# A new order for the first stage of an attention and mixture-of-experts layer, with routing spread over the shared expert by a table

## The chip, the core and the metric

The kernel runs on one core of a Trainium2 chip. The metric is the time of one execution on the device, in microseconds (us), as the median of several runs. PE is TensorE, DVE is VectorE, ACT is ScalarE, POOL is GpSimd and SP is SyncE, which here only issues DMAs. Each engine executes its own queue in order, and waits in it on semaphores.

## The reference

```python
xn = layernorm(x)                       # x is 4 x 1024 tokens of 256
z = softmax((xn@Wq.T + bq) @ (xn@Wk.T + bk).T / 16) @ (xn@Wv.T + bv)      # per batch
gates = softmax(xn @ Wg.T)              # 16 experts, the best 2 chosen, their scores normalised
y = sum over the 2 of score * ((silu(xn@We_gate.T) * (xn@We_up.T)) @ We_down.T)   # hidden 128
shared = (silu(xn@Ws_gate.T) * (xn@Ws_up.T)) @ Ws_down.T                   # hidden 512
out = x + z + y + sigmoid(xn@Wsg.T) * shared
```

## The kernel before

The 4096 tokens are 32 tiles of 128 and 8 chunks of 512 tokens (4 tiles). All wide products are made in three passes: each operand is split in a rounded part (HI, a copy by ACT) and the remainder (LO, a subtraction, `remainder`, by DVE), and PE multiplies HI by HI, HI by LO and LO by HI.

There are three stages. **Stage one** is the shared expert of all 8 chunks, with the layer norm, the routing, and the splitting of all expert weights beside it. **Stage two** takes 40 pairs of blocks of 128 tokens, each block for one expert; it begins when PE starts line 847 (`blk_gate_up`, 0). **Stage three** is the attention, with the scattered results of the experts gathered and added. The change touches the first stage and small things that follow from it.

`plan()` writes out one list of steps, and each engine's program walks it and executes its own share of each step. So a step's place in the list is its place in all queues. The steps of stage one are:

- `stats c`: DVE's statistics of a chunk's 4 tiles; `root`, `invert`: DVE and ACT make the reciprocal deviation, for the groups of chunks in `ROOTS`; `norm c`: the normalised tiles, two by POOL and two by ACT (chunk 0: two by DVE), which SP also stores to the tensor `rows`.
- `tokens_in c`: PE transposes the chunk (8 transposes, banks 0 and 1), ACT and DVE split the result into `xT`; SP stores it as `keys` at the step `logits c`.
- `logits c`: PE's router product (4 matmuls of 512 columns), ACT copies it out; `logits_turn c`: PE transposes it back, all into bank 7; `best_experts q` (two chunks each): DVE copies and adds the two halves, then `max` and `max_index` of 8 tiles.
- `gate_up c,j` (j from 0 to 3): two products, 12 matmuls of 512 columns, into banks 2 and 3 or 4 and 5; ACT takes the silu of the one, DVE multiplies it by the other (line 1195); `hidden c,j`: ACT (HI) and DVE (LO, line 1123) split it into `hT`. `down c,m`: 24 matmuls of 256 columns, and DVE adds the result (line 1209). The loop over these is called the shared sequence here, 48 parts; (c,j) is one of them.
- `row_shift`: 12 matmuls of one column from Wq and the biases; `shared_weights n`: the split of 512 columns of the shared weights.
- `chosen`, `counts`, `ranks`, `slot_sums`, `slots`, `slot_parts`: from the chosen experts to each token's slot, a chain between DVE and PE. `slot_hots g`: for 4 tiles, DVE compares the slots' places and blocks with a range (`place_hot`, `block_hot`, lines 1301 and 1297), POOL multiplies `block_hot` by the token numbers (line 623), and `rows_map g` on PE multiplies the two; 8 groups. Then the block's rows are known, and POOL may gather them (`blk_load`).
- `expert_split n`: HI by ACT, LO by DVE; SP loads expert n+2 when the LO of n is done (two staging buffers).

In the version before the order follows from rules (`expert_next`, `map_next`, `shared_next`): the logits steps and best experts stand between two parts, the routing chain behind (3,1), and an expert split behind each `gate_up` from then on, all 16 LO parts on DVE. The first `gate_up` stands behind two chunks of `tokens_in` and four of the six weight splits.

Of the kernel before, what the change touches and what calls it, by code (L numbers as in the profile page):

```python
# [18 lines left out]
P = 128  # L19
# [26 lines left out]
def shape_constants():  # L46
# [17 lines left out]
        (P * np.arange(TILES)[None, :] + p[:, None] - MIDDLE).astype(np.float32),  # L64
# [5 lines left out]
ORDER = [*range(4), *range(12, NE), *range(4, 12)]  # L70

AWAY = range(2, 6)
QT = TILES // 4
PER = P // NE
ROOTS = ((0,), (1,), (2, 3), (4, 5, 6, 7))


def plan():


    steps, held, unsplit, unmapped = [], [], list(range(NE)), list(range(-1, MAPS + 1))
    known = {"slots": False, "blocks": False}
# [5 lines left out]
    def expert_next(c):  # L88
        if not unsplit or not known["slots"]:
            return  # L90
        expert = ORDER[unsplit[0]]
        if expert >= 12:
            now = known["blocks"]
        elif expert >= 10:
            now = not unmapped
        elif expert >= 8:
            now = c > 5
        elif expert >= 6:
            now = c > 4
        elif expert >= 4:  # L100
            now = c > 3
        else:
            now = True
        if now:
            steps.append(("expert_split", unsplit.pop(0)))
# [20 lines left out]
    def shared_next():  # L126
        part, c, n = shared.pop(0)
        part(c, n)

    def map_next():  # L130
        g = unmapped.pop(0)
        if 0 < g:
            steps.append(("rows_map", g - 1))
        if g + 1 < MAPS:
            steps.append(("slot_hots", g + 1))
        if not unmapped:
            steps.append(("rows_known",))

    def normed_root(*chunks):
        steps.append(("root", *chunks))  # L140
        steps.append(("invert", *chunks))

    steps.append(("stats", 0))
    normed_root(0)
    steps += [("norm", 0), ("stats", 1)]
    normed_root(1)
    steps += [("norm", 1), ("tokens_in", 0), ("row_shift",), ("shared_weights", 0), ("shared_weights", 1), ("stats", 2),
              ("shared_weights", 2), ("shared_weights", 3), ("stats", 3), ("tokens_in", 1)]
    normed_root(2, 3)
    steps += [("norm", 2), ("logits", 0), ("shared_weights", 4), ("shared_weights", 5)]  # L150
    shared_next()
    steps += [("logits_turn", 0), ("logits", 1)]
    for c in range(2, NCH + 1):
        if c < NCH:
            steps.append(("tokens_in", c))
        if c < 4:
            steps += [("stats", 2 * c), ("stats", 2 * c + 1)]
        if c == 3:
            normed_root(4, 5, 6, 7)
        if c + 1 < NCH:  # L160
            steps.append(("norm", c + 1))
        shared_next()
        if c > 2:
            steps.append(("logits", c - 1))
        shared_next()
        steps.append(("logits_turn", c - 1))
        if c % 2 == 0:
            steps.append(("best_experts", c // 2 - 1))
    steps.append(("chosen",))
    shared_next()  # L170
    shared_next()
    steps += [("counts",), ("expert_load", 0), ("expert_load", 1)]
    shared_next()
    steps += [("ranks",), ("slot_sums",)]
    shared_next()
    steps += [("slots",), ("slot_parts",)]
    known["slots"] = True
    for n in range(6):
        shared_next()
        if n % 2 == 0:  # L180
            map_next()
    steps += [("row_slots",), ("experts_of_blocks",), ("pair_scores",)]
    known["blocks"] = True
    while shared:
        shared_next()
        if unmapped:
            map_next()
        if shared:
            shared_next()
    while unsplit:  # L190
        expert_next(NCH)
    assert not unmapped

    steps += [("blk_load", b) for b in range(XR)]
    steps += [("blk_turn", 0), ("blk_turn", 1), ("down", NCH - 1, 0), ("down", NCH - 1, 1), ("qkv_load",)]
# [38 lines left out]
class Places:  # L234
# [3 lines left out]
    def __init__(self, steps):  # L238
# [4 lines left out]
        ring, turn, summed = 0, 0, False  # L243
        for step in steps:
            kind = step[0]
            banks = []
            if kind == "tokens_in":
                banks = [(("turn", (turn + k) % 2), (*step, k)) for k in range(KD)]
                turn += KD
            elif kind in ("logits", "rows_map"):  # L250
# [6 lines left out]
            elif kind == "down":  # L257
                banks = [(("down", step[2] if summed else 0), step)]
            elif kind == "slot_sums":
# [33 lines left out]
def build(nc, x, bv, Wqkv, bqk_in, Wr, We, Ws, const_f, const_b, out):  # L293
# [4 lines left out]
    with ctx:  # L298
# [206 lines left out]
        def inverse_of(c):  # L505

            return 5 * [c in group for group in ROOTS].index(True) + 4
# [17 lines left out]
        def sync_program(e):  # L525
# [10 lines left out]
            for c in range(3):  # L536
                load_x(c)
# [928 lines left out]
```

## Time and profile before

| | us |
|---|---|
| median of 3 runs (592.13 to 593.46) | 592.26 |
| the profiled execution's own time | 590.49 |
| its span, from the first to the last instruction | 588.7 |
| PE busy in the span | 542.5 |
| DVE busy in the span | 378.6 |
| start of stage two (PE line 847) | 209.04 |

The span leaves out what lies around the instructions (1.8 us here). Busy times are sums of an engine's instructions; PE's are modelled at their ends. Stages two and three are executed by the same code before and after the change.

### The profile page before, as it was taken

The numbers are of one execution on the slowest core, as the hardware profiler recorded it, in microseconds if no ns is written. First come the engines' busy times: TensorE is split into PE (matmuls) and PEld (weight loads), VectorE is DVE, ScalarE is ACT, GpSimd is POOL, SyncE is SP. The second block draws the span as 40 slices with busy tenths as digits, with TensorE's granted clock in tenths as the row PEclk, the third lists the DMA queues.
The fourth block names the chain that finished last, engine by engine and source line by source line (L and its number), as shares of the span: only waits on it lengthen the run. The fifth ranks groups of instructions, "written<-read, shape, count | busy, mean of one in ns | idle before, by whom it ended". The sixth has DMA issues, their size and how long they took to land.

```text
span 588.7 us, 10343 instructions
## 1 busy us (share of the span) xinstructions
PE 542.5 (92%) x3660; PEld 492.3 (84%) x3661; DVE 378.6 (64%) x798; ACT 233.3 (40%) x409; POOL 183.0 (31%) x174
## 2 busy tenths in 40 slices
PE   1595999797999999999999999999999999999997
PEld 1474878576888899999999889889888989889986
DVE  4576564689887557566665566665666656665665
ACT  3354442141454336555554533333333333333331
POOL 2123300012333467577760202222222222222222
PEclk9998999999899999999999999999999999999999
DMA  8752453012314156496676901115111111112112
GB/s 303 247 215 99 186 225 117 1 36 73 106 55 144 47 162 189 153 316 211 189 144 154 330 28 46 47 53 188 53 55 50 49 46 46 55 45 64 55 60 67
DMA packets 35600, 69.30 MB, mean 118 GB/s; under 512 B 4960, under 2 KB 17632, under 8 KB 34528
## 3 DMA queue, kind: packets, MB, share of 16 engines
q1 hardware_dynamic: 28064, 49.42, 23.8%
q0 software_dynamic: 6912, 18.88, 12.5%
q8 instruction: 31, 0.51, 0.4%
q10 hardware_dynamic: 576, 0.35, 0.2%
q14 instruction: 17, 0.14, 0.1%
HBM read 41.37 MB, written 27.26 MB: 117 GB/s over the span
## 4 chain that ended last, share of the span: by engine, by line
PE 80%; DVE 13%; ACT 3%; issue 2%; DMA 1%; POOL 0%; DVEq 0%; ACTq 0%
PE ps L669 46%; PE ps L847 10%; PE ps L791 7%; PE ps L868 5%; PE ps L675 5%; PE ps L923 5%; DVE bn_stats_out L1130 2%; PE ps L747 1%; DVE sil L1195 1%; DVE idx L1173 1%; DVE pT L1123 1%; DVE nmax L1403 1%; DMA acc<-in_x 1%; ACT vv L944 1%; DVE hT L1123 1%
## 5 line engine op out<-in xcount | busy, mean ns | idle before, releaser
L656 POOL DMA_INDIRECT rows_y<-ytab,slot x64 | 64.8, 1013 | 209.6 <-DVE acc L1432 179.5
L669 PE MATMUL ps<-xT,shared_w 128*128 128x512 f32 x384 | 96.2, 406 | 5.8 <-DVE sil L1195 5.8
L642 POOL DMA_INDIRECT blk_x<-rows,row x80 | 82.0, 1025 | 51.3 <-issue 26.4
L669 PEld LDWEIGHTS ps<-vv,pT 128*128 128x128 f32 x768 | 95.9, 192 | 1.9
L669 PE MATMUL ps<-vv,pT 128*128 128x256 f32 x768 | 97.0, 283 | 0.0
L669 PEld LDWEIGHTS ps<-xT,shared_w 128*128 128x128 f32 x384 | 74.2, 197 | 22.4 <-issue 6.0
L669 PE MATMUL ps<-xbT_hi,qT 128*128 128x512 f32 x256 | 87.5, 403 | 0.0
L1110 ACT ACTIVATE probs_f<-ps,less 128x1024 f32<-128x1024 f32 x32 | 35.7, 1115 | 103.8 <-DVE less L1406 103.8
L847 PE MATMUL ps<-expert_w,blk_xT 128*128 x480 | 66.6, 288 | 0.0
L847 PEld LDWEIGHTS ps<-expert_w,blk_xT 128*128 128x128 f32 x480 | 59.7, 190 | 0.1
L669 PEld LDWEIGHTS ps<-xbT_hi,qT 128*128 128x128 f32 x256 | 48.1, 188 | 9.4
L791 PE MATMUL ps<-shared_w,hT 128*128 128x256 f32 x384 | 48.5, 285 | 3.4 <-DVE slot_tmp L1251 2.5
L791 PEld LDWEIGHTS ps<-shared_w,hT 128*128 128x128 f32 x384 | 46.9, 191 | 4.1 <-DVE slot_tmp L1251 2.6
L669 PE MATMUL ps<-xbT_lo,qT 128*128 128x512 f32 x128 | 50.0, 390 | 0.0
L944 ACT ACTIVATE pT<-ps 128x1024 fp32r<-128x1024 f32 x32 | 32.8, 1026 | 42.3 <-PE ps L923 42.3
L1123 DVE TENSOR_TENSOR pT<-ps,pT 128x1024 fp32r<-128x1024 f32 x32 | 39.1, 1223 | 14.9 <-ACT pT L944 14.7
L1403 DVE TENSOR_REDUCE nmax<-ps 128x1 f32<-128x1024 f32 x32 | 39.1, 1222 | 10.4 <-PE ps L669 10.4
L623 POOL TENSOR_TENSOR block_hot<-block_hot,token 128x640 f16<-128x640 f16 x8 | 17.3, 2160 | 87.1 <-DVE block_hot L1297 87.1
L944 ACT ACTIVATE hT<-sil 128x512 fp32r<-128x512 f32 x32 | 19.4, 628 | 62.0 <-PE ps L791 32.9
L1123 DVE TENSOR_TENSOR blk_xT<-ps,blk_xT 128x512 fp32r<-128x512 f32 x40 | 27.5, 690 | 20.0 <-ACT blk_xT L944 19.9
L868 PE MATMUL ps<-expert_w,blk_hT 128*128 x240 | 38.5, 296 | 0.1
L923 PE MATMUL ps<-cf,probs_f 128*128 128x128 f32 x256 | 34.3, 277 | 4.3 <-ACT probs_f L1110 4.3
(148 smaller groups left out, 813.0 us busy)
## 6 DMA issues: line engine op xcount, KB each, us to landing
ytab<-blk_y SPq DMA_DIRECT2D x40, 256.0 KB, 3.0
keys<-xT SPq DMA_DIRECT2D x8, 1024.0 KB, 5.2
stage_e<-in_experts SPq DMA_DIRECT2D x16, 384.0 KB, 3.0
acc<-in_x SPq DMA_DIRECT2D x8, 512.0 KB, 9.0
rows<-xn SPq DMA_DIRECT2D x8, 512.0 KB, 3.0
xbT_hi<-keys SPq DMA_DIRECT2D x8, 512.0 KB, 7.3
xbT_lo<-keys SPq DMA_DIRECT2D x8, 512.0 KB, 8.4
out<-acc SPq DMA_DIRECT2D x32, 128.0 KB, 1.7
```

The lines of the kernel that those rows point to most:

```text
L642: e.indirect_dma_start(out=blk_x[:, q, n, :], out_offset=None, in_=rows, in_offset=bass.IndirectOffsetOnAxis(ap=row[:, 2 * b + n:2 * b + n ...
L656: e.indirect_dma_start(out=rows_y[:, r, k, :], out_offset=None, in_=ytab, in_offset=bass.IndirectOffsetOnAxis(ap=slot[:, k, i:i + 1], axis=0),
L669: ins = e.matmul(dst, stationary(p, k), moving(q, k), start=(n == 0), stop=(n == total - 1))
L675: ins = e.transpose(dst[:, n * P:(n + 1) * P], s, ident)
L791: ins = e.matmul(ps[:, b, (n % 2) * D:(n % 2 + 1) * D], hT[:, p, j, n * P:(n + 1) * P], shared_w[:, q, 2 * KD * SH + j * D:2 * KD * SH + ( ...
L847: ins = e.matmul(ps[:, 2 + r, n * D:(n + 1) * D], blk_xT[:, r, p, (n * KD + k) * P:(n * KD + k + 1) * P], weights(b, n, q, k * 2 * HID, 2 ...
L868: ins = e.matmul(ps[:, 6 + r, n * D:(n + 1) * D], blk_hT[:, r, p, n * P:(n + 1) * P], weights(b, n, q, 2 * D, D), start=(at == 0), stop=(a ...
L923: ins = e.transpose(ps[:, 4 + k // CT, (k % CT) * P:(k % CT + 1) * P], probs_f[:, n % 2, k * P:(k + 1) * P], ident)
L944: e.activation(hi, src, ACT.Copy).then_inc(done, 1)
L1110: e.activation(probs_f[:, w, :], ps[:, b0:b0 + 2, :].rearrange("p a b -> p (a b)"), ACT.Exp, bias=less[:, w:w + 1], accum_out=lsum[:, w:w ...
L1123: e.tensor_tensor(lo, src, hi.bitcast(F32), ALU.subtract).then_inc(done, 1)
L1403: e.tensor_reduce(nmax[:, w:w + 1], ps[:, b0:b0 + 2, :], mybir.AxisListType.XY, ALU.max, negate=True).then_inc(max_found, 1)
```

## The change

The order of stage one is written out as a table, `beside`, of what follows each of the 48 parts of the shared sequence. Parts of chunk 0 are followed by their `hidden` at once. The shared weights come in the order of `gate_up` (512 columns of gate and up for each j), and are loaded and split one by one; the first two chunks of work start behind one chunk of `tokens_in` and one split. Chunk 0 of x comes in two halves. Tokens are laid out so that a partition holds 4 consecutive ones of a chunk. The norm of chunks 1 to 7 gives one tile to POOL and three to ACT. `logits_turn` uses a bank of the pair 0 and 1, ACT copies and DVE adds per chunk; `counts` and `ranks` use these banks too, `down` has bank 6 for m=0 and bank 7 for m=1. Expert splits begin beside (1,3), and 11 of the 16 LO parts are POOL's (`ON_POOL`). POOL's multiplication of `block_hot` goes; DVE makes it in 8 `tensor_scalar` instructions of 80 columns a group, 64 in all. Two DVE conversions of slots go.

```diff
-ORDER = [*range(4), *range(12, NE), *range(4, 12)]
+ORDER = (0, 1, 2, 3, 4, 5, 12, 6, 13, 7, 15, 8, 9, 14, 10, 11)
+ON_DVE = (5, 9, 11, 13, 15)
+ON_POOL = tuple(n for n in range(NE) if n not in ON_DVE)
...
-        if j >= 2 or (c, j) == (0, 1):
+        if j >= 2 or c == 0:
             hidden_held()
-        expert_next(c)
...
+    steps += [("row_shift",), ("stats", 0), ("weights_hi", 0), *root_of(0), *inverse(0), ("norm", 0), ("weights_lo", 0),
+              *tokens(0), *weights(1), ("stats", 1), *root_of(1)]
+    beside = {
+        0: [*inverse(1), ("norm", 1), ("shift_copied",), *weights(2)],
+        1: [("router_split",), *weights(3), ("logits", 0), ("stats", 2)],
+        2: [("logits_turn", 0), *tokens(1)],
+        3: [("logits", 1), ("stats", 3)],
+        4: [("logits_turn", 1), ("best_experts", 0)],
+        5: [*weights(4), *weights(5), *root_of(2), *inverse(2), ("norm", 2)],
+        6: [("stats", 4), ("expert_load", 0), ("expert_load", 1)],
+        7: [*tokens(2)],
+        8: [("logits", 2), ("norm", 3), ("stats", 5)],
+        9: [("logits_turn", 2), *tokens(3), *splits(0)],
+        10: [("logits", 3), ("stats", 6)],
+        11: [("logits_turn", 3), ("stats", 7), *root_of(3)],
+        12: [*inverse(3), ("norm", 4), *splits(1)],
+        13: [*tokens(4), ("norm", 5)],
+        14: [("logits", 4), ("best_experts", 1)],
+        15: [("logits_turn", 4), *tokens(5), ("norm", 6), *splits(2)],
+        16: [("logits", 5), ("norm", 7)],
+        17: [("logits_turn", 5), *tokens(6), *splits(3)],
+        18: [("logits", 6), ("best_experts", 2)],
+        19: [("logits_turn", 6), *tokens(7), *splits(4)],
+        20: [("logits", 7)],
+        21: [("logits_turn", 7)],
+        22: [("best_experts", 3)],
+        23: [("choices",), ("hot", 0), ("hot", 1)],
+        24: [("counts",)],
+        25: [("ranks",), *splits(5)],
+        26: [("slot_sums",), *splits(6)],
+        27: [("slots", 0)],
+        28: [("slots", 1), ("slot_parts",), *splits(7)],
+        29: map_hots(0),
+        30: [*mapped(0), *map_hots(1), *splits(8)],
+        31: [*mapped(1), *splits(9)],
+        32: map_hots(2),
+        33: [*mapped(2), ("blocks", 0), *splits(10)],
+        34: map_hots(3),
+        35: [*mapped(3), *map_hots(4)],
+        36: [*mapped(4), *map_hots(5)],
+        37: [*mapped(5), *splits(11)],
+        38: [("blocks", 1), *splits(12)],
+        39: map_hots(6),
+        40: [*mapped(6), *map_hots(7)],
+        41: [*mapped(7), ("rows_known",), ("row_slots",), ("pair_scores",), *splits(13)],
+        42: splits(14),
+        43: splits(15),
+    }
...
-        rows_t = rows.rearrange("(i p) d -> p i d", p=P)
+        rows_t = rows.rearrange("(c p n) d -> p c n d", p=P, n=CT)
-        x_t = x.rearrange("(i p) d -> p i d", p=P)
-        out_t = out.rearrange("(i p) d -> p i d", p=P)
+        x_t = x.rearrange("(c p n) d -> p c n d", p=P, n=CT)
+        out_t = out.rearrange("(c p n) d -> p c n d", p=P, n=CT)
...
+            e.dma_start(acc[:, 0:CT // 2, :], x_t[:, 0, 0:CT // 2, :]).then_inc(x_loaded_half, 16)
+            e.dma_start(acc[:, CT // 2:CT, :], x_t[:, 0, CT // 2:CT, :]).then_inc(x_loaded[0], 16)
+            e.dma_start(shift_w[:, :, :], Wqkv[:, 0, :].rearrange("p (k d) -> p k d", d=D)).then_inc(shift_loaded, 16)
+            load_gate_up(0)
+            load_gate_up(1)
+            load_x(1)
+            load_gate_up(2)
+            load_gate_up(3)
+            load_x(2)
...
-                elif kind == "slot_hots":
-                    e.wait_ge(block_hot_found, g + 1)
-                    e.tensor_tensor(found.rearrange("p i k b -> p i (k b)"), found.rearrange("p i k b -> p i (k b)"),
-                                    tokens.unsqueeze(2).to_broadcast([P, MAPPED, TOPK * BLOCKS]),
-                                    ALU.mult).then_inc(block_hot_made, 1)
+                elif kind == "expert_split" and a[0] in ON_POOL:
+                    n = a[0]
+                    e.wait_ge(expert_hi, n + 1)
+                    e.tensor_tensor(expert_w[:, ORDER[n], LO, :], stage_e[:, n % 2, :],
+                                    expert_w[:, ORDER[n], HI, :].bitcast(F32), ALU.subtract).then_inc(expert_lo_p, 1)
...
-                    e.tensor_tensor(block_hot[:, g % 2, :, :],
-                                    places16[:, 0:BLOCKS].unsqueeze(1).to_broadcast([P, MAPPED * TOPK, BLOCKS]),
-                                    blk.unsqueeze(2).to_broadcast([P, MAPPED * TOPK, BLOCKS]),
-                                    ALU.is_equal).then_inc(block_hot_found, 1)
+                    for n in range(MAPPED * TOPK):
+                        i, k = MAPPED * g + n // TOPK, n % TOPK
+                        e.tensor_scalar(block_hot[:, g % 2, n, :], places16[:, 0:BLOCKS], slot_blk[:, k, i:i + 1],
+                                        token[:, i:i + 1], ALU.is_equal, ALU.mult).then_inc(block_hot_made, 1)
```

The 48 parts are numbered from 0: chunk 0 has parts 0 to 3, and chunk c from 1 on the six from 6c-2: (c,0), (c,1), down (c-1,0), down (c-1,1), (c,2), (c,3). The last two are down (7,0) and (7,1), ahead of which stand the loads and transposes of the first blocks, as before.

## Rows read from the trace of the kernel before

**Rows 1.** Length, busy time of PE, PEld, DVE, ACT, POOL; clock, DMA share, GB/s.

```profile
9.73:209.04 199.31, 171.48 (x992) 145.42 (x994) 139.37 (x379) 78.85 (x140) 48.75 (x36) 0.97 0.36 126
...
123.00:177.00 54.00, 48.48 (x308) 41.21 (x307) 49.30 (x73) 21.47 (x35) 17.28 (x8) 0.97 0.24 75
209.00:324.00 115.00, 114.89 (x977) 114.10 (x976) 71.62 (x146) 61.12 (x143) 68.93 (x68) 1.00 0.66 192
```

**Rows 2.** Waits of PE up to 240 us: in total, times, longest.

```profile
PE ps L675 <- ACT xn L965: 9.7, 1, 9.7
PE ps L747 <- DVE xT L1123: 8.7, 3, 5.9
PE ps L669 <- DVE sil L1195: 5.8, 3, 4.4
```

**Rows 3.** Timeline of PE: start, us, line, tiles, count, idle before.

```profile
71.82 2.89 PE L669 MATMUL ps<-xT,shared_w 128*128 128x512 f32 x12
74.64 0.46 PE L760 MATMUL ps<-cf,logits_t 64*128 64x64 f32 x4
75.03 1.09 PE L675 MATMUL ps<-cf,xn 128*128 128x128 f32 x8
...
79.62 2.88 PE L669 MATMUL ps<-xT,shared_w 128*128 128x512 f32 x12
...
125.60 5.93 PE L669 MATMUL ps<-xT,shared_w 128*128 128x512 f32 x24 [1.09 <-DVE sil L1195]
...
148.23 7.33 PE L669 MATMUL ps<-xT,shared_w 128*128 128x512 f32 x24 [4.43 <-DVE sil L1195]
...
155.70 5.99 PE L791 MATMUL ps<-shared_w,hT 128*128 128x256 f32 x48
...
209.04 1.60 PE L847 MATMUL ps<-expert_w,blk_xT 128*128 x12
```

**Rows 4.** Timeline of DVE: a part's two operations, map comparisons, expert splits.

```profile
75.20 0.69 DVE L1195 TENSOR_TENSOR sil<-sil,ps 128x512 f32<-128x512 f32 x1 [1.94 <-PE ps L669]
76.58 0.69 DVE L1123 TENSOR_TENSOR hT<-sil,hT 128x512 fp32r<-128x512 f32 x1 [0.70 <-ACT hT L944]
...
130.76 0.82 DVE L1297 TENSOR_TENSOR block_hot<-places,slot_blk 128x640 f16<-128x640 f16 x1
131.49 1.22 DVE L1301 TENSOR_TENSOR place_hot<-places,slot_place 128x1024 f16<-128x1024 f16 x1
132.63 0.68 DVE L1195 TENSOR_TENSOR sil<-sil,ps 128x512 f32<-128x512 f32 x1
133.23 1.41 DVE L1123 TENSOR_TENSOR expert_w<-stage_e,expert_w 128x768 fp32r<-128x768 f32 x1
...
149.52 0.96 DVE L1123 TENSOR_TENSOR expert_w<-stage_e,expert_w 128x768 fp32r<-128x768 f32 x1
```

**Rows 5.** Timeline of POOL.

```profile
29.60 3.36 POOL L514 TENSOR_SCALAR xn<-acc,moments,rstd 128x256 f32<-128x256 f32 x2
...
131.65 2.17 POOL L623 TENSOR_TENSOR block_hot<-block_hot,token 128x640 f16<-128x640 f16 x1 [5.68 <-DVE block_hot L1297]
```

**Rows 6.** Timeline of DVE: short instructions, two and eight in a row.

```profile
8.37 0.73 DVE L514 TENSOR_SCALAR xn<-acc,moments,rstd 128x256 f32<-128x256 f32 x2
...
43.43 0.71 DVE L1170 MAX8 top<-logits_sb 128x8 f32<-128x16 f32 x8
```

**Rows 7.** Timeline of ACT: a table load ahead of its instruction.

```profile
44.64 1.28 ACT L956 ACT_TABLE_LOAD   x1
```

**Rows 8.** Stretches of best experts, chosen, slot sums, slots and their parts.

```profile
83.88:86.00 2.12, 2.12 (x11) 1.73 (x10) 2.08 (x27) 1.79 (x4) 0.00 (x0) 1.00 0.95 398
103.50:105.65 2.15, 1.18 (x6) 0.64 (x4) 2.12 (x8) 0.00 (x0) 0.00 (x0) 1.00 0.00 0
110.50:113.00 2.50, 0.00 (x0) 0.00 (x0) 2.23 (x7) 0.00 (x0) 0.00 (x0) 1.00 0.00 0
117.00:120.95 3.95, 3.95 (x27) 3.58 (x26) 3.74 (x13) 1.15 (x2) 0.00 (x0) 1.00 0.00 0
```

More of the change, by code:

```diff
@@ L153, in plan @@
[L153 to L195, printed above, removed]
+    shared += [(down, NCH - 1, 0), (down, NCH - 1, 1)]
+    def root_of(group):
+        return [("root", *ROOTS[group])]
+    def inverse(group):
+        return [("invert", *ROOTS[group])]
+    def tokens(c):
+        return [("tokens_in", c)]
+    def weights(n):
+        return [("weights_hi", n), ("weights_lo", n)]
@@ new lines, in splits, with map_hots, mapped @@
+    def splits(*numbers):
+        return [("expert_split", n) for n in numbers]
+    def map_hots(g):
+        return [("slot_hots", g)]
+    def mapped(g):
+        return [("rows_map", g)]
+    steps += [("row_shift",), ("stats", 0), ("weights_hi", 0), *root_of(0), *inverse(0), ("norm", 0), ("weights_lo", 0),
[46 more added lines that the diff above has]
+    }
@@ L196, in plan @@
+    for n, (part, c, m) in enumerate(shared):
+        if n + 2 == len(shared):
+            steps += [("blk_load", b) for b in range(XR)] + [("blk_turn", 0), ("blk_turn", 1)]
+        part(c, m)
+        steps += beside.get(n, [])
+    steps.append(("qkv_load",))
     beside = {5: ("qkv_split", 0), 6: ("qkv_split", 1), 7: ("qkv_split", 2), 9: ("mix", 0), 10: ("mix", 1),
@@ L246, in __init__ @@
             banks = []
[L247 to L250, printed above, removed]
+            if kind in ("tokens_in", "ranks"):
+                banks = [(("turn", (turn + k) % 2), (*step, k)) for k in range(2)]
+                turn += 2
+            elif kind in ("logits", "logits_turn", "counts", "rows_map"):
                 banks = [(("turn", turn % 2), step)]
@@ L500, in build @@
         TURNS = KD * NCH
[L501 removed]
+        ROUTED = {"ek": 2, "gap": 3, "hot": 6, "totals": 7, "summed": 14, "slots": 18, "blocks": 21}
         Y_LAST = 16 * (PAIRS // XR)
@@ L507, in inverse_of, with chunks_of, staged, split_waits @@
             return 5 * [c in group for group in ROOTS].index(True) + 4
+        def chunks_of(chunks):
+            return slice(CT * chunks[0], CT * chunks[-1] + CT)
+        def staged(n):
+            return stage_gu[:, n, :] if n < SJ else stage_d[:, n - SJ, :]
+        def split_waits(e, last):
+            for done, made in ((expert_lo_p, ON_POOL), (expert_lo_v, ON_DVE)):
+                n = sum(1 for m in made if m <= last)
+                if n:
+                    e.wait_ge(done, n)
         def xT_of(c):
@@ L796, in tensor_program @@
                 elif kind == "counts":
+                    bank = turn_bank(("counts",))
                     e.wait_ge(const_b_loaded, 32)
```

370 lines of the change are left out of this document (160 added, 210 removed).

## The prediction, made before the changed kernel was run

> **What bounds the kernel now.** I read three views, in this order. The stretches of the span first [rows 1]: from 209 to 324 us, stage two, PE is busy 114.89 of 115.00 us, so a change in the first stage can give it nothing; the gain or loss is the time at which stage two starts, 209.04 [rows 3], and what follows moves along with it. From the first transposes at 9.7 to there, PE is busy 171.5 of 199.3 us: 27.8 are idle, and some of the busy time is at the lower clock. The waits of PE say on what [rows 2]: 9.7 us before the first transposes, 8.7 on the LO part of xT (the first router products, which stand behind statistics and weight splits), 5.8 on DVE's multiplication of a part. Then DVE alone: from 123 to 177 us, while the row maps are made, it is busy 49.3 of 54.0 us, more than PE's 48.5 [rows 1]. So the first third of the stage is bound by chains between ACT, DVE and PE, and the last part by DVE's queue, with PE just behind it.
>
> **How the sum is made.** I walked the new table of steps in queue order with durations from the rows. On PE a part (c,j) costs 2.8 (71.82 to the next start at 74.64), a `down` 2.9 (half of 5.99, less the overlap at its end), a turn back of logits 0.4 (74.64 to 75.03), a chunk's transposes 0.85 (1.09, less the same overlap), a router product 0.9, a third of a part's twelve matmuls [rows 3]. On DVE a multiplication and a LO part take 0.6 each of the queue, and a part with its `hidden` behind it 2.0, since 0.7 of that is a wait for ACT's HI copy (75.20 to 76.58, then 0.6) [rows 4]; best experts 2.1, chosen 2.1, slot sums 2.4, slots and their parts 3.7 of 3.95 without the two conversions that go [rows 8]; a place comparison 1.14 (131.49 to 132.63) and a LO part of an expert 0.9 [rows 4].
>
> **First third, up to (2,0).** Before, (2,0) begins at 79.62 [rows 3]. Now `row_shift` is done on PE while the statistics are made (below nothing: it cost 3 us between chunks), the norm of chunk 0 ends about 0.3 earlier since x comes in halves (bounds 0 and 0.8, half a chunk's landing), and the first part can start behind one chunk of transposes and one split: about 12.7. It doesn't run on: ACT and DVE do `hidden` 0, invert and norm 1, the shift and weights 2 before the silu of (0,1), and the router's split after that, so PE idles from about 20 to 25.6 for the router's LO part. I get (0,2) at 27, (0,3) at 34, (1,0) at 37.5, (1,1) at 41, a wait of 2 for weights 4 and 5 before down (0,0) at 46, (1,2) at 52.7 and (2,0) at 62.6. The old order had then done more of the routing: three chunks of transposes (2.6), three router products (2.8) and two turns (0.8), 6.1 us. So the order gains 79.6 - 62.6 - 6.1 = 10.9 here.
>
> **Middle, (2,0) to (4,0).** Nine parts, four `down`s and the rest of tokens and logits are 46 us of PE. The new stalls come from the shared banks: the transposes of a chunk follow the turn back of the logits of the last one, and their second bank waits until DVE has added that turn back, which stands behind the part's LO. That costs 2.2 before (2,0) (counted), 3.6 + 1.0 at chunks 5 and 4, 0.3 at 6 and 1.6 at 7. The 3.6 has the table load in it: ACT loads a table as soon as the instruction is at the head of its queue, 1.28 us [rows 7]; roots 2 and 3 apart instead of fewer groups cost one pair of loads more. (4,0) comes out at 113.9, against 125.60 [rows 3].
>
> **Last part, (4,0) to stage two.** DVE's work: of 16 expert splits 11 go to POOL, 11 x 0.9 = 9.9 off (all 16 had stood behind (4,0)). Added: chosen, counts, ranks, slot sums, slots and parts were done before (4,0) and come after it now, 2.1 + 0.7 + 2.4 + 3.7 = 8.9. The `block_hot` comparison (0.73 of the queue, 130.76 to 131.49 [rows 4]) becomes eight of 80 columns. No row has that instruction. Two neighbours: 256 columns by two operations with scalars take 0.73 - 0.41 = 0.32 each in a row, 16 columns 0.08 [rows 6]; on the line between them 80 columns take 0.14, 1.15 a group and 3.3 more for the 8 groups. Bounds: 0.08 each, a gain of 0.7 in all, and 0.20, a loss of 7. Walking this in order, PE waits 2.6 for the first map, 1.8 for the third, 0.8 for the fourth, 2.8 for the seventh, and stage two starts at 200.1. The same by totals: 9.9 saved against 12.2 added, plus what PE itself has more, gives 125.6 - 113.9 = 11.7 less 2.8, so 8.9 earlier than 209.04.
>
> **POOL's new work, and its price for DVE.** POOL's nearest row for two inputs is 2.17 us for 640 columns, or 2.6 scaled to 768; as DVE's place comparison was executing until 1.1 before its end, it may itself have waited, so the lower bound is 1.3. I take 2. ACT is idle enough and SP's next load (3 us) has a part or two of time, so POOL's lateness costs nothing itself. But the port does: an expert's LO part on DVE took 1.41 instead of 0.96 when it came up at 133.23 while POOL's instruction lasted to 133.82, and ended 0.82 behind that [rows 4, 5]; the other way, of POOL's two norms at 29.60 (3.36 for two of 1.2) one lost 0.9 to DVE's two subtractions. Multiplications that read PSUM didn't wait. In my order DVE's SBUF work meets POOL at four splits: slot sums (1.8), slots (0.6), hots 1 (0.2) and the blocks' comparison (1.9). Of these 4.5 I let PE see 3. The Trainium skill says the same in SBUF — State Buffer, "Who interferes with whom": a DVE instruction with two SBUF inputs and a GpSimd instruction that reads SBUF exclude each other for the whole instruction. The trace agrees with its 0.45. GPSIMD Engine Reference, section 3.1, has 4497 ns for 2048 columns of this subtraction's kind; an estimate from it is 1.7 us for 768, and the 3 above would be 2.5 by it.
>
> **The clock.** Where PE idled 4.43 before 148.23, its next two parts took 7.33 instead of 5.93 [rows 3]. Three of my stalls are 2.6 to 4.6 long; where DVE is late anyway, the slower products are hidden. I charge 1, bounds 0 and 4.
>
> **Sum.** 8.9 - 3 - 1 = 4.9 gained. On the profiled execution that is 590.5 - 4.9 = 585.6; its time is 1.8 below the median shown, on which it would be 587.4. I say 586. The new layout of tokens leaves gathers and stores with rows of 1 KB; I cost it at nothing (cover: stage two's loads run ahead of PE, as its 114.9 of 115 shows; without cover the 40 pairs would each show it).
>
> **The rivals.**
> *Better, the queue isn't late* (0.22): if the small comparisons take 0.08, POOL's meetings fall into DVE's idle 0.7 us gaps and the bank waits are shorter, then only about 5 of the 16.6 us of waits I walked remain behind (2,0): 590.5 - 8.9 - 6 = 576 to 581. For it: my walk puts every instruction at its full latency. Against: DVE had 5 us to spare in 54 before, and gets no lighter.
> *Given back* (0.12): the first third is as forecast, but small comparisons at 0.20 (3.7 more) and the bank waits bring DVE so late that stage two starts within 2 us of before: 588.5 to 592.
> *The port decides, slower* (0.14): if each of the six POOL splits between (4,2) and the last map holds DVE for its whole 2.6, that is 15.6, of which PE sees all but the 2.6 of two that fall on slack: 13 instead of 3, 590.5 - 8.9 + 1 + 13 = 595.6. It decides against the change from 8 us in all, 1.3 each. For it: the 1.41 row. Against: more than half of DVE's instructions read PSUM, and the lock is seen only when they meet.
> *As forecast* (0.52): 582 to 590.
>
> **The numbers.** A difference of 0.3%, 1.8 us, is what a measurement of this kernel can tell. Faster holds the better case and nearly all of the forecast: 0.74. Same is the given-back case: 0.12. Slower is the port's: 0.14. The range reaches from 577 to 593: it leaves out the upper half and more of the port's case (0.12), and the lowest end of the better one (0.05).
>
> **What would show it.** In the new profile: the first part before 14 us; PE waiting for the router's LO part once, about 5; (2,0) near 63; `xT` transposes waiting on DVE's adds; the eight-in-a-row at 0.14 each; DVE over 90% busy between the first and the last map; DVE's subtractions over 1 us only where a POOL subtraction is executing; stage two at 200 to 206, and its length unchanged at 115. I am wrong if PE's waits behind the first map are gone (better), if stage two starts after 207 (given back, port), or if stages two and three change their length.

## The result, and the profile of the changed kernel

The changed kernel takes 602.67 us (median of 4 runs, 599.18 to 604.92) where the kernel before takes 592.19 on the same chip (4 runs, 591.92 to 593.46): a ratio of 1.0167, 95% interval 1.0114 to 1.0221. It is slower by 1.7%, and the forecast was 586 with a range that ended at 593. The profiled execution took 601.69, with a span of 599.6.

I read the views in the order of [rows 1 to 4]. First the stretches (us, busy time and instructions of PE, its weight loads, DVE, ACT and POOL, then the granted clock):

```profile
9.73:219.84 210.11, 176.67 (x983) 148.66 (x983) 141.50 (x423) 85.75 (x157) 42.42 (x28) 0.93 0.33 118
66.00:120.00 54.00, 47.61 (x262) 39.99 (x263) 29.81 (x111) 29.56 (x55) 15.02 (x9) 0.94 0.43 150
120.00:200.00 80.00, 65.75 (x383) 55.35 (x383) 65.61 (x174) 21.27 (x37) 10.49 (x5) 0.91 0.17 56
137.00:197.00 60.00, 45.95 (x273) 38.85 (x271) 51.50 (x119) 16.59 (x27) 10.49 (x5) 0.91 0.17 53
219.84:333.00 113.16, 113.13 (x965) 112.48 (x964) 70.56 (x144) 60.83 (x142) 70.83 (x71) 1.00 0.69 195
```

Stage two starts at 219.84 instead of 209.04, and from there PE is busy 113.13 of 113.16 us; what remains to the end of the span is 379.8 in this kernel and 379.7 in the one before. So the whole difference, 10.8, is in stage one, as the argument said it would be, with the other sign. Against [rows 1], 5.6 of it is idle time of PE (33.4 instead of 27.8) and 5.2 is busy time (176.67 instead of 171.48). PE has not been given more to do, so the 5.2 is a sign of the clock: granted 0.93 on average instead of 0.97. The page of the profile says the same of the whole execution: 7.8 more busy time than before (542.5) in the same 3660 matmuls. DVE is busy 51.50 of the 60 us in which the maps are made, 86%, where I had named over 90% as a sign of my walk being right: its queue has gaps there.

```profile
PE 550.3 (92%) x3660; PEld 498.0 (83%) x3661; DVE 380.3 (63%) x841; ACT 240.4 (40%) x426; POOL 178.9 (30%) x169
```

PE's waits up to the start of stage two, which answer to [rows 2]:

```profile
PE ps L825 <- DVE block_hot L1312: 12.6, 6, 4.8
PE ps L677 <- DVE logits_sb L1176: 7.7, 4, 2.6
PE ps L740 <- POOL bq_wide L625: 7.3, 1, 7.3
PE ps L754 <- DVE router L1132: 5.4, 1, 5.4
PE ps L794 <- issue: 2.1, 1, 2.1
```

The 8.7 on xT and the 5.8 on the multiplication are gone. In their place are 12.6 for the maps' `block_hot`, and 7.7 for the addition of the logits that were turned back, which the next chunk's second bank waits for. PE's own timeline shows what happens behind such a wait (a group of neighbours, its start and length, and in brackets the idle time before it; this answers to [rows 3]):

```profile
13.57 8.15 PE L671 MATMUL ps<-xT,shared_w 128*128 128x512 f32 x24 [1.41 <-DVE xT L1132]
27.15 2.08 PE L754 MATMUL ps<-xT,router 128*128 128x512 f32 x4 [5.43 <-DVE router L1132]
29.03 4.48 PE L671 MATMUL ps<-xT,shared_w 128*128 128x512 f32 x12
...
48.41 7.48 PE L794 MATMUL ps<-shared_w,hT 128*128 128x256 f32 x48 [2.10 <-issue]
...
66.25 0.86 PE L677 MATMUL ps<-cf,xn 128*128 128x128 f32 x4 [2.10 <-DVE logits_sb L1176]
66.76 4.47 PE L671 MATMUL ps<-xT,shared_w 128*128 128x512 f32 x12
...
71.98 2.88 PE L671 MATMUL ps<-xT,shared_w 128*128 128x512 f32 x12
...
95.27 3.92 PE L671 MATMUL ps<-xT,shared_w 128*128 128x512 f32 x12
...
120.94 5.76 PE L671 MATMUL ps<-xT,shared_w 128*128 128x512 f32 x24
...
154.55 0.69 PE L825 MATMUL ps<-block_hot,place_hot 128*128 128x80 f16 x8 [4.83 <-DVE block_hot L1312]
155.04 4.71 PE L794 MATMUL ps<-shared_w,hT 128*128 128x256 f32 x24
...
168.03 0.45 PE L825 MATMUL ps<-block_hot,place_hot 128*128 128x80 f16 x8 [2.43 <-DVE block_hot L1312]
168.30 7.33 PE L671 MATMUL ps<-xT,shared_w 128*128 128x512 f32 x24
...
196.98 4.24 PE L671 MATMUL ps<-xT,shared_w 128*128 128x512 f32 x12
```

The reader is to compare groups of equal count. Twelve matmuls of a part take 2.88 at 71.98, 4.47 at 66.76 and 3.92 at 95.27; a pair of `down`s takes 7.48 at 48.41 where it took 5.99 in [rows 3]; two parts take 7.33 instead of 5.76. Each long one stands behind a wait. The granted clock of the stretch of such a group and of one at full speed:

```profile
66.76:71.00 4.24, 4.24 (x14) 3.38 (x13) 0.69 (x1) 1.93 (x3) 1.83 (x1) 0.63 0.01 4
71.98:74.70 2.72, 2.72 (x13) 2.06 (x11) 1.75 (x9) 1.19 (x2) 0.00 (x0) 1.00 0.99 377
```

A mean of 0.63 says that PE had half its clock for most of the first group, and all of it in the second. Part (2,0) begins at 66.76 and (4,0) at 120.94, where I had 62.6 and 113.9.

On DVE, the small comparisons come in eights, and five instructions are longer than their kind. Two of them, the first a small one:

```profile
139.25 1.84 DVE L1253 TENSOR_SCALAR nblk_i<-nblk_i 128x16 int32<-128x16 int32 x1
...
150.28 2.43 DVE L1306 TENSOR_TENSOR place_hot<-places,slot_place 128x1024 f16<-128x1024 f16 x1
152.64 1.76 DVE L1312 TENSOR_SCALAR block_hot<-places,slot_blk,cf 128x80 f16<-128x80 f16 x8
```

```profile
139.22 1.84 POOL L630 TENSOR_TENSOR expert_w<-stage_e,expert_w 128x768 fp32r<-128x768 f32 x1 [21.70 <-ACT expert_w L950]
...
149.83 1.80 POOL L630 TENSOR_TENSOR expert_w<-stage_e,expert_w 128x768 fp32r<-128x768 f32 x1 [2.28 <-ACT expert_w L950]
```

Eight comparisons hold the queue for 1.68 (152.64 to 154.32), so 0.21 each in a row. POOL's subtraction takes 1.8, and both long instructions of DVE overlap with one.

### The profile page after: what moved, and what is told of

It is laid out like the page before. It is cut to its first block, busy times and chain, and to the rows that moved or that the text cites. A ratio compares the mean times of both kernels' runs of the same rounds, so it can differ in the third digit from the quotient of the medians.

```text
span 599.6 us, 10421 instructions
## 1 busy us (share of the span) xinstructions
PE 550.3 (92%) x3660; PEld 498.0 (83%) x3661; DVE 380.3 (63%) x841; ACT 240.4 (40%) x426; POOL 178.9 (30%) x169
## 4 chain that ended last, share of the span: by engine, by line
PE 76%; DVE 13%; ACT 5%; issue 4%; DMA 1%; SPq 0%; DVEq 0%; ACTq 0%
PE ps L671 44%; PE ps L853 10%; PE ps L677 5%; PE ps L794 5%; PE ps L874 5%; PE ps L929 5%; DVE sil L1208 2%; ACT hT L950 2%; DVE block_hot L1312 2%; DVE hT L1132 2%; PE ps L754 1%; DVE place_hot L1306 1%; DMA stage_gu<-in_shared 1%; ACT xn L970 1%; DVE pT L1132 1%
## 5 line engine op out<-in xcount | busy, mean ns | idle before, releaser
L671 PE MATMUL ps<-xT,shared_w 128*128 128x512 f32 x384 | 102.0, 422 | 2.8 <-DVE xT L1132 1.4
L671 PEld LDWEIGHTS ps<-xT,shared_w 128*128 128x128 f32 x384 | 77.9, 207 | 20.7 <-DVE sil L1208 1.8
L630 POOL TENSOR_TENSOR expert_w<-stage_e,expert_w 128x768 fp32r<-128x768 f32 x11 | 21.6, 1967 | 115.2 <-ACT expert_w L950 115.2
L794 PE MATMUL ps<-shared_w,hT 128*128 128x256 f32 x384 | 52.0, 296 | 2.4 <-issue 2.1
L794 PEld LDWEIGHTS ps<-shared_w,hT 128*128 128x128 f32 x384 | 50.1, 203 | 3.3 <-issue 2.5
L1208 DVE TENSOR_TENSOR sil<-sil,ps 128x512 f32<-128x512 f32 x32 | 21.9, 684 | 28.9 <-PE ps L671 26.8
L874 PE MATMUL ps<-expert_w,blk_hT 128*128 x240 | 38.5, 296 | 0.1
```

The lines of the kernel that those rows point to most:

```text
L671: ins = e.matmul(dst, stationary(p, k), moving(q, k), start=(n == 0), stop=(n == total - 1))
L794: ins = e.matmul(ps[:, b, (n % 2) * D:(n % 2 + 1) * D], hT[:, p, j, n * P:(n + 1) * P], shared_w[:, q, 2 * KD * SH + j * D:2 * KD * SH + ( ...
L874: ins = e.matmul(ps[:, 6 + r, n * D:(n + 1) * D], blk_hT[:, r, p, n * P:(n + 1) * P], weights(b, n, q, 2 * D, D), start=(at == 0), stop=(a ...
L1208: e.tensor_tensor(sil[:, r, :], sil[:, r, :], ps[:, 3 + 2 * r, :], ALU.mult).then_inc(hidden, 1)
```

## The experiments

In each diff and expectation the names are those of the change; some diffs are given in short form. The first four ran on one chip, where the kernel before took 593.32. The other eight ran on chips where it took 610.34 and 610.33, so across these calls only ratios to it are compared, and places in stage one. Ratios stand with their 95% interval. In some of the later versions the first matmuls of stage two come early and trickle in between others; so there I give a mark behind these, which counts their waits in: the first product of the experts' second layer (PE L874 in the changed kernel). It stands at 229.09 in the changed kernel when run on such a chip (changed_again, below), and at 225.38 in its first profile. Each trace is of one execution, so a difference of marks of 2 or 3 us between two kernels alone shows little. From the mark to the end of the span it is 389 to 392 us in all eight of them (374.2 in the changed kernel's first profile, so the slower chips lose most of their time behind stage one).

### Which part of the change costs

**wide_hot** takes the 64 small comparisons back out (in short form; a conversion of the slots' blocks and one of the token numbers come with it):

```diff
-for n in range(8): tensor_scalar(block_hot[n], places16[:, 0:80], slot_blk[n], token[n], is_equal, mult)   # DVE
+tensor_tensor(block_hot, places16[:, 0:80] (broadcast), slot_blk16 (broadcast), is_equal)                   # DVE, 640 columns
+tensor_tensor(block_hot, block_hot, token16 (broadcast), mult)                                            # POOL
```

> The changed kernel with the old block comparison: one DVE instruction of 640 columns a group and POOL's multiplication by the token numbers, in place of DVE's eight of 80. Theory 1 (the small instructions are the loss: 0.21 of DVE's queue each, 1.68 a group instead of 0.73, 7.6 us in all, of which PE's 12.6 us of waits for them hold most): 592 to 596 instead of 602. Theory 2 (POOL's two-input instructions hold DVE): POOL gets 8 more of them, so no faster than 600. Theory 3 (the order's own waits and the lower clock behind them): 1 to 3 us faster at most, above 599.

Measured: 1.0155 [1.0137, 1.0172], stage two at 220.59. Within the intervals that is the changed kernel's own ratio: the theory by which the small comparisons are the loss fails.

**dve_splits** gives all LO parts of experts back to DVE:

```diff
-ON_DVE = (5, 9, 11, 13, 15)
+ON_DVE = tuple(range(NE))
```

> The changed kernel with all 16 LO parts of the experts on DVE. Theory 2: DVE loses 5.2 us of holds (139.25, 146.97, 150.28, 190.97 and 202.79 in the profile after) and gets 11 x 0.9 = 9.9 us of work, part of it at times when it idles; if the holds on the critical stretch are what costs, 598 to 602. Theory 1 (DVE's queue as a sum): 6 to 9 us slower, 608 to 611. Theory 3: a change of under 2 us either way.

Measured: 1.015 [1.0126, 1.0175], stage two at 220.56. Again nothing changes, so POOL's new work isn't the loss either, net of what it takes off DVE.

**order_only** makes both edits, so that the new order, loads and banks are what remains.

> Both undone: the new order, banks, layout and loads alone, with the old block comparison and all expert splits on DVE. Theory 1: DVE has the same work as before the change, and the order gives 8 to 11 us in the first third: 583 to 590. Theory 3: the order itself is slow through PE's waits on banks and the clock: 597 or more.

Measured: 1.0109 [1.0075, 1.0144], stage two at 220.13. The order with its banks and loads is slow by itself, 1.1% slower than the kernel before. (The trace is of the slowest of its four executions, 602.93 with a median of 600.58.) It shows why the comparison in one piece doesn't help:

```profile
149.78 0.82 DVE L1323 TENSOR_TENSOR block_hot<-places,slot_blk 128x640 f16<-128x640 f16 x1
150.52 1.22 DVE L1327 TENSOR_TENSOR place_hot<-places,slot_place 128x1024 f16<-128x1024 f16 x1
```

```profile
150.75 2.10 POOL L635 TENSOR_TENSOR block_hot<-block_hot,token 128x640 f16<-128x640 f16 x1 [55.21 <-DVE block_hot L1323]
```

```profile
152.99 0.53 PE L840 MATMUL ps<-block_hot,place_hot 128*128 128x80 f16 x8 [4.34 <-POOL block_hot L635]
```

From the first comparison to the map it is 3.2 here (149.78 to 152.99). With the eight small ones it is the same where POOL is out of the way: in the changed kernel's third group from 164.97 (DVE's comparison of places) to the map at 168.03, 3.1. PE's waits at the maps add up to 13.4 here against 12.6. DVE isn't short of time at these maps: ahead of the comparisons of the fourth group it idles 1.8 in this trace (until 171.29). Ahead of the first map it has almost no gap from 142.0 on, so in that wait of 4.34 its queue has a part as well.

**small_hot_in_before** puts the small comparisons alone into the kernel before, and takes POOL's multiplication out there.

> The kernel before with nothing but the eight small comparisons a group (and POOL's multiplication gone). Theory 1: 64 x 0.21 - 8 x 0.73 = 7.6 us of DVE's queue, in a stretch where DVE was busy 49.3 of 54: 4 to 8 us slower, 596 to 600. Theory 3: under 2 us slower.

Measured: 1.0068 [1.0047, 1.0089], stage two at 213.84 instead of 209.04.

```profile
151.66 7.88 PE L657 MATMUL ps<-xT,shared_w 128*128 128x512 f32 x24 [6.57 <-DVE sil L1183]
```

```profile
133.20 1.78 DVE L1290 TENSOR_SCALAR block_hot<-places,slot_blk,cf 128x80 f16<-128x80 f16 x8
```

There DVE's queue is what binds, and PE reads the delay at once: the wait that was 4.43 in [rows 3] is 6.57, and the two parts behind it take 7.88. A group costs 1.70 of the queue instead of 0.73, 7.8 for the eight, of which 4.8 arrives at stage two.

### Where the order loses: maps, turns, clock

**map_later** moves each map one step further behind its comparisons; the expert splits keep their steps:

```diff
-        30: [*mapped(0), *map_hots(1), *splits(8)],
-        31: [*mapped(1), *splits(9)],
-        32: map_hots(2),
-        33: [*mapped(2), ("blocks", 0), *splits(10)],
+        30: [*map_hots(1), *splits(8)],
+        31: [*mapped(0), *splits(9)],
+        32: [*mapped(1), *map_hots(2)],
+        33: [("blocks", 0), *splits(10)],
+        34: [*mapped(2), *map_hots(3)],
... (and so on to mapped(7) at 42)
```

> The changed kernel with each rows_map (and rows_known, row_slots and pair_scores with it) a part or two behind its place in the table, so that DVE has a part more for the group's comparisons. Theory A (the table's places make PE wait: a group's map stands one part behind its comparisons, 12.6 us of waits in the profile after, the slow matmuls behind them 5 more): 588 to 594. Theory B (DVE's queue is the bound in this stretch, so the wait only moves from the map to the next part): 600 to 603.

Measured: 1.009 [1.0061, 1.0119], 0.8 to 1.0% below the changed kernel, which is 5 to 6 us. The profiled execution is the fastest of the four (612.45 with a median of 615.08). In it the maps' waits fall from 12.6 to 7.0, and the granted clock from 120 to 200 us is 1.00 instead of 0.91. The mark comes at 220.79, 8.3 earlier. DVE's queue is late next: in those 80 us it is busy 70.9 instead of 65.6.

**turn_later** lets a chunk's transposes go ahead of the turn back of the logits before it, for chunks 1, 3, 5, 6 and 7, so that they wait for no addition, and moves the first router product a part further behind the router's split:

```diff
-        2: [("logits_turn", 0), *tokens(1)],
-        3: [("logits", 1), ("stats", 3)],
+        2: [("logits", 0), *tokens(1)],
+        3: [("logits_turn", 0), ("logits", 1), ("stats", 3)],
...
-        9: [("logits_turn", 2), *tokens(3), *splits(0)],
-        10: [("logits", 3), ("stats", 6)],
+        9: [*tokens(3), *splits(0)],
+        10: [("logits_turn", 2), ("logits", 3), ("stats", 6)],
```

> The changed kernel with the turn back of the logits a part later, behind the next chunk's transposes (chunks 0, 2, 4, 5, 6), and the first router product a part later. PE's 7.7 us of waits on the add of the turned logits and its 5.4 on the router's LO part should go. Theory A (each such wait is lost time, as nothing in this stretch is bound by DVE): 9 to 13 us less with the slow matmuls, 590 to 594. Theory B (the time comes back in the map stretch, where DVE's routing chain starts from the last best experts): 597 to 602.

Measured: 0.9978 [0.995, 1.0007], stage two at 208.64, the mark at 216.05, 13.0 earlier. All 7.7 of waits on the logits' addition are gone, and with them the low clock: from 66 to 120 us it is 1.00 instead of 0.94. The 5.4 for the router's LO part have become 3.4 for that of the third split of shared weights (weights 2, which part (0,2) needs). The waits at the maps stay: 13.8.

**fill** shortens no chain. PE gets work that nobody needs where it would wait, so that only its clock can change. In short form:

```diff
+def fill(bank, n):
+    for _ in range(n):
+        e.matmul(ps[:, bank, :], shared_w[:, HI, 0:P], shared_w[:, HI, 0:BANK], start=True, stop=True)
...
+    fill(bank, 14)     # before the wait for the router's LO part
+    fill(6, 8)         # before the first down of chunk 0
+    fill(2, 8)         # before the second bank of tokens 3; 10 before that of tokens 5
+    fill(bank, 18)     # before map 0; 9, 4 and 15 before maps 2, 3 and 6
```

The results of these matmuls are not used. Nothing of the kernel is left out.

> The changed kernel with matmuls added on PE that nobody reads, in front of the waits of the profile after: 14 before the router's LO part, 8 before the last weight splits, 8 and 10 before the second bank of chunks 3 and 5, 18, 9, 4 and 15 before maps 0, 2, 3 and 6. They shorten no wait. Theory C (a good part of the loss is PE at its lower clock behind the waits; 12 us more than at the higher one, by the rows over 2.9 for a part): 592 to 597. Theory D (PE's rate behind a wait is hidden by DVE's lateness): 600 to 606.

Measured: 1.0016 [1.0002, 1.0029], stage two at 212.69. The changed kernel stands at 1.0167 and, run again, at 1.0188 (changed_again, below), so 1.5 to 1.7%, or 9.2 to 10.5 us, come back for waits whose length was left as it was. The stretches and PE's timeline of this kernel:

```profile
66.00:120.00 54.00, 50.17 (x287) 41.72 (x286) 31.00 (x113) 30.38 (x58) 15.03 (x9) 1.00 0.47 173
120.00:200.00 80.00, 74.29 (x468) 63.08 (x469) 70.17 (x183) 22.09 (x36) 14.69 (x8) 1.00 0.14 42
```

```profile
145.09 4.27 PE L727 MATMUL ps<-shared_w 128*128 128x512 f32 x18
150.18 0.45 PE L835 MATMUL ps<-block_hot,place_hot 128*128 128x80 f16 x8 [0.82 <-DVE block_hot L1322]
150.46 3.11 PE L803 MATMUL ps<-shared_w,hT 128*128 128x256 f32 x24
...
159.77 2.20 PE L727 MATMUL ps<-shared_w 128*128 128x512 f32 x9
162.37 0.45 PE L835 MATMUL ps<-block_hot,place_hot 128*128 128x80 f16 x8 [0.40 <-DVE block_hot L1322]
162.64 5.72 PE L671 MATMUL ps<-xT,shared_w 128*128 128x512 f32 x24
```

From the first filler to the map it is 5.1 (145.09 to 150.18), much as the 4.83 that PE idled there in the changed kernel, but what follows takes 3.11 instead of 4.71, and 5.72 instead of 7.33. The granted clock is 1.00 from 66 us on. So the clock is worth 7.2 us of the start of stage two against the first profile (219.84) and 9.2 against the second (221.87); the mark, at 220.12, says 5.3 and 9.0.

Where the time comes back can be followed in the two timelines of PE, fill against the first profile: it is 0.1 ahead at the first `down` (48.32 against 48.41), 1.7 at (2,0), 4.4 at (4,0), 5.7 behind map 1 (154.21 against 159.88) and 7.2 at stage two. Each step is at a group that was slow and is no longer. Nothing comes back before the first `down`: there PE still waits 2.27, behind 14 idle matmuls, and 1.49, where it has none, and the parts that follow, at 27.34 and 34.80, still take 4.50 and 4.49.

The Trainium skill has this in TensorE: Matmul & The Clock Gate, "HAM oscillation — how this bites in real kernels": idle gaps of PE in a loop bring its clock down to half, and the work behind them pays. The trace agrees in kind: twelve matmuls of 2.88 take 4.47 behind a wait of 2.10, at a mean granted clock of 0.63.

**all_later** puts map_later and turn_later together, and the first split of shared weights behind the norm of chunk 0:

```diff
-    steps += [("row_shift",), ("stats", 0), ("weights_hi", 0), *root_of(0), *inverse(0), ("norm", 0), ("weights_lo", 0),
+    steps += [("row_shift",), ("stats", 0), *root_of(0), *inverse(0), ("norm", 0), ("weights_hi", 0), ("weights_lo", 0),
```

> Both moves together, and the first copy of shared weights behind the first norm instead of ahead of its root (in the profile after ACT waits for that load until 7.21, and the first norm is no earlier than in the kernel before). Theory A: the gains add, 580 to 586, below the kernel before. Theory B: not below 592; DVE's queue is the bound.

Measured: 0.989 [0.9862, 0.9918], the mark at 209.93, 19.2 earlier. The two gains nearly add up (8.3 and 13.0 at the mark). This is the first version that is faster than the kernel before, by 1.1%.

### The repeat, and what is left

**changed_again** is the changed kernel without an edit, on the chip of the three runs below.

> The changed kernel itself, beside the kernel before on the same chip as the three below, since the absolute times of the last runs were 18 us above those of the first. A ratio of 1.014 to 1.019 if the loss is the first stage's alone (10.8 us later in the profiles) and doesn't depend on the chip.

Measured: 1.0188 [1.0135, 1.024], stage two at 221.87, the mark at 229.09. PE's waits and the clock are nearly those of the first profile (12.6, 7.7, 0.94 and 0.91): 13.8 at the maps, 7.6 for the logits' addition, 0.91 and 0.92 from 66 to 120 and from 120 to 200 us.

**later_wide** is all_later with the wide comparison of wide_hot.

> The all_later kernel with the old block comparison and POOL's multiplication. Its profile has DVE without a gap from the first map's comparisons to the last's, and 1.68 us a group in the small instructions, so if DVE's queue binds now, 8 x 0.95 less is worth 4 to 7 us: a ratio of 0.978 to 0.983. If maps are bound by POOL's 2.2 us behind the comparison or by its holds of DVE, as wide_hot had no gain, the ratio stays at 0.987 to 0.991.

Measured: 0.982 [0.9793, 0.9846], the mark at 205.69, 4.2 before that of all_later. **later_dve_splits** is all_later with all LO parts on DVE.

> The all_later kernel with all expert LO parts on DVE. In the changed kernel that cost nothing, because PE waited anyway. If DVE's queue is the bound once the places are mended, 10 splits x 0.9 us less the 5 us of holds by POOL come through: 3 to 6 us slower than all_later, a ratio of 0.994 to 1.000. If the holds cost as much as the work saved, 0.989 again.

Measured: 0.9834 [0.9789, 0.9879], the mark at 208.66, 1.3 before that of all_later. The edit to the comparisons, which gave nothing in the changed kernel, now gives 0.7%, clear of noise. For the splits it is 0.6%, but the interval overlaps with that of all_later and 1.3 at the mark is little, so a gain isn't shown. The stretch from 137 to 187 us in all_later says what had changed:

```profile
137.00:187.00 50.00, 41.31 (x281) 34.28 (x280) 47.14 (x116) 13.86 (x24) 8.42 (x4) 1.00 0.15 45
```

With the maps out of PE's way, DVE is busy 47.1 of 50 us (94%), and what the wide comparison spares its queue PE gets. That the kernel gains nothing from POOL's splits, though they take 9.9 off DVE's queue, fits with DVE being held when it meets them: in all_later one `place_hot` takes 2.48 instead of 1.22. The whole price of these meetings was not isolated.

**later_wide_fill** is later_wide with idle matmuls at two places, and only there:

```diff
+    fill(bank, 9)      # before the wait for the third split of shared weights, part (0,2)
+    fill(6, 8)         # before the first down of chunk 0
```

> later_wide with 9 matmuls that nobody reads before the third part of chunk 0 and 8 before the last weight splits, where all_later has PE waits of 3.4 and 2.1 us and slow matmuls behind them (4.59 and 7.47 instead of 2.9 and 5.9). If PE's rate there is worth its time, 2 to 3 us less than later_wide; if ACT and DVE set the pace of chunk 0, the same within 1 us.

Measured: 0.9746 [0.9717, 0.9774], the mark at 202.77: 594.52 us where the kernel before takes 610.33 and the changed one 621.91 on the same chip. Its PE timeline, and behind it that of later_wide, in which the same two places have no filler:

```profile
24.31 3.01 PE L686 MATMUL ps<-xT,shared_w 128*128 128x512 f32 x12 [1.36 <-DVE shared_w L1154]
...
43.54 6.02 PE L816 MATMUL ps<-shared_w,hT 128*128 128x256 f32 x48 [0.24 <-DVE shared_w L1154]
```

```profile
23.79 4.44 PE L686 MATMUL ps<-xT,shared_w 128*128 128x512 f32 x12 [3.38 <-DVE shared_w L1147]
...
43.37 7.48 PE L809 MATMUL ps<-shared_w,hT 128*128 128x256 f32 x48 [2.10 <-issue]
```

The two groups take 2.9 less, and the mark comes 2.9 earlier, but that the two agree is chance. What the first group saves is gone at the `down` (43.54 against 43.37), which waits for the last split of the weights. Only the `down`'s 1.5 lasts, less 0.2: from there on PE is 1.3 ahead, up to stage two (195.09 against 196.41). The other 1.6 arise among the first blocks of stage two, whose products trickle in and run partly at the lower clock in later_wide, and 2.2 more lie behind the mark in these two traces (the medians differ by 4.7). No filler stands there, and no run shows why. This is the best version that was found, 2.5% faster than the kernel before and 4.4% faster than the changed one.

## Why the prediction was wrong

The step that failed is the term for the clock, "I charge 1, bounds 0 and 4". The row for it was there ([rows 3], 7.33 behind a wait of 4.43), and the walk had found the waits (besides the three that it counted for the clock, the 5 for the router's LO part and the 2 for weights 4 and 5), but then priced every group of matmuls behind them at full speed and argued that "where DVE is late anyway, the slower products are hidden". They are not hidden: where PE has become the late one, its slowness makes the next silu, and so DVE's queue, late too. The fill run measures the term at 7.2 to 9.2. The trace's own slow groups say where it arises: 1.1 for the router product at 27.15 (2.08 for 0.9 to 1.0), 1.7 for the `down`s at 48.41, 1.6 at 66.76, 1.0 at 95.27, and 1.7, 1.6 and 1.4 behind maps 0, 2 and 6, together 10.1, and 1.6 more for the part at 29.03. Fill brought back 7.1 of the 9.0 that lie from the first `down` on, and nothing before it.

The other steps, with forecast and measured start of stage two 15.7 apart (204.1, which is 209.04 less 4.9, and 219.84):

- **Small comparisons.** 0.14 each was charged, 0.21 was measured, over the upper bound of 0.20: 0.53 a group more, 4.3 for the eight groups. In the kernel before they cost 4.8 alone, and taking them out of all_later gave 4.2 at the mark. But wide_hot shows that nothing is saved in the changed kernel by going back to one wide comparison, since the chain through POOL is as long. So what this term costs in the changed kernel itself no run shows.
- **Waits.** PE waits 12.6 for maps where the walk had 2.6 + 1.8 + 0.8 + 2.8 = 8.0; the 4.6 more are near the 4.3 of the comparisons, though with the wide comparison, in order_only, it is 13.4. For the banks 7.7 instead of about 8.7. For the router's LO part 5.43 where I had "about 5". These mechanisms were right.
- **Slips.** From (2,0) to (4,0) there are eight parts, not the nine that I wrote. And of DVE's instructions it isn't more than half that read PSUM: from 123 to 177 us of the kernel before it is 26 of 73.
- **First third.** The first part starts at 13.57, not 12.7. Chunk 0's norm didn't end earlier but 0.5 later: ACT stood at the split of the first shared weights, and waited 3.59 for their load, with the root of the statistics behind it. But that isn't all: all_later takes this split away from there, its norm runs at 7.46 instead of 8.99, and its first part still starts at 13.46. What stands in the way then is `row_shift`, which I had "done on PE while the statistics are made": PE waits 7.3 and 7.5 in the two kernels for the biases' load and POOL's copy of them, and it is done with `row_shift` only at about 10, where the transposes begin (10.22, and 10.10 in all_later). The 0.9, with 1.1 and 1.7 of slow clock, is most of the 4.2 by which (2,0) is late.
- **The port.** Five meetings held DVE for 5.2 us in all, 3.7 of it before the last map (4.5 and 3 were forecast). The rival in which it decides didn't occur, and dve_splits, where no split is POOL's, is no faster. POOL's subtraction is 1.85 (2 was taken).
- **The sum.** Only the clock's term is measured by a run in this kernel; the others are differences of durations from what I had. The clock's 7.2 to 9.2 less the 1 charged, with 4.3, 0.7 and 0.9 from the other three, is 12 to 14 of the 15.7; 2 to 4 remain without an owner.
- **Rivals.** Of my signs of being wrong one occurred, stage two after 207, and I had it point to "given back" or "port". No rival had the clock as its mechanism. With the walk's gain of 8.9 and the port's 3, a clock bound at 10 instead of 4 would have reached 595, beyond the range but still short of the 601.69 of the profiled execution; it takes the comparisons and the first third's start as well to come within 2 to 4 us of it.

Why the order itself doesn't gain is then plain. It does bring (4,0) 4.7 earlier than before (120.94 against 125.60), but 8.9 of routing that had been done by then is still to do. PE's four bank waits and six map waits add up to 20.3, and most of the long ones are followed by matmuls at the low clock. That theory was tested from both sides: fill gives the clock back and leaves the waits, turn_later and map_later shorten the waits.

## What to carry to other kernels

When a walk of a new order finds a wait on the engine that binds, price what stands behind it at the slow rate that the same trace shows behind its own waits, and let this be a rival by itself. In an order written out by hand, an instruction that consumes the end of a chain belongs a full step behind it; moving the maps and turns by one step, with one split of weights, was worth 2.9% here, while the edits that had looked expensive were worth nothing until that was done. Taking work out of a queue pays only where that queue is what the bound engine waits for, so try such an edit again after the order is mended. Filler in front of a wait pays only if what follows doesn't end in another wait: of the two places in later_wide_fill one paid.

## What the runs showed of the hardware beyond what I had expected

**Short waits can lower the clock, and length alone doesn't tell which.** Behind 2.10 of idle time twelve matmuls took 4.47 instead of 2.88; behind 2.53 in the kernel before, a pair of `down`s took its usual 6.02; in all_later the part behind map 0's wait of 2.05 took its usual 2.99. Even the same wait in the same kernel goes both ways: behind 2.43 ahead of map 2 two parts took 7.33 in the changed kernel's first profile, behind 2.44 they took 5.73 in changed_again. In fill the clock stays at 1.00 from 66 us on, but behind its first filler a wait of 2.27 still lowered it.

**A small comparison costs more than its columns say.** One of 80 columns of f16, with two scalars by pointer, lasts 0.29 to 0.30 and follows the one before by 0.21. Whether the pointers are what costs was not tried. The Trainium skill's VectorE: DVE Perf Modes, "The TRN2 errata — SBUF-src ops pay a fixed extra latency per instruction", says that many small tiles each pay a fixed cost that one large tile pays once, and its formula, without an acceleration by a faster mode, gives an estimate of 0.14 for this one. The trace agrees in kind (eight of 80 columns hold the queue for 1.68, one of 640 for 0.73), and the measured 0.21 decides.

**POOL can hold a tiny instruction of one input.** An int32 `tensor_scalar` of 16 columns took 1.84 beside POOL's subtraction of 1.84, and 0.17 in dve_splits, where POOL had no subtraction. My forecast had 1.8 of holding at the slot sums, but my reason for it was DVE's instructions with two inputs. SBUF — State Buffer, "Who interferes with whom" in the Trainium skill, names this case too: copies, casts and `tensor_scalar` can enter a mode that takes the shared ports. The trace agrees: this `tensor_scalar` has 16 columns, began 0.03 after POOL's instruction and ended with it (141.09 and 141.06).
